# A Mamba layer with a mixture of experts: x * Dskip moves from a VectorE operation per half into the PSUM sum as a diagonal matmul

## The chip, the cores and the metric

The kernel runs on one core of a Trainium2 chip. The metric is the device time in microseconds. All operands are fp32 in memory. Besides the transfers there are four engines to follow: TensorE (PE in the profile, PEld for its weight loads), VectorE (DVE), ScalarE (ACT) and GpSimd (POOL).

## The reference

The input is (32, 256, 128), 8192 tokens. It is layer-normalised to xn, and the result is `x + mamba(xn) + moe(xn)`. Of the mamba part, this is what matters here (256 inner channels in two halves of 128, 16 states per channel):

```python
x = silu(conv(x) + conv_b)                    # xs in the kernel
delta = softplus(dt_proj(x_proj(x)) + dt_proj_b)
s = s * exp(delta * A) + (delta * x) * B      # a scan over 256 tokens
y = sum over the 16 states of s * C
y = y + x * Dskip
y = y * silu(z)                               # zs in the kernel
out = y @ out_proj_w.T
```

The mixture of experts sends each token to one of eight experts (128 to 512 to 128) and weighs it by its gate.

## The kernel before

After a start of some 95 us (weights, layernorm, routing) one loop runs over 16 chunks of 512 tokens, and in each over 32 slots, 16 to a half of the channels. The order of work on every engine is written out by hand: the tables `STAGE_A`, `OUT_PROJ`, `FFN_AT`, `SOFTPLUS` and `GATE` name the slots at which a piece of work is issued or read. Nothing is planned at run time; an engine does its list in order and waits at semaphores.

In slot w of a chunk:

- TensorE spreads the rows of du and delta over the partitions for slot w + 2, with one fp32r matmul each (`spread_du`, L1186, into `du_ps`, and `spread_delta`, L1193, into `decay`). The first waits until VectorE has read the bank's earlier content, the second until the scan of slot w - 1 is done. Behind them in its list come the sums over the states and the tiles of other work of that slot.
- ScalarE turns the spread delta into a decay with Exp (L808). Between these it does the SiLUs of the next chunk (L709, L711, each pair with two table loads), its softplus (L731 to L745) and the evacuations of the experts' tiles (L762, L768, L774, L784).
- VectorE multiplies the spread du by B (`spread_u`, L926) one slot ahead and scans (L991).
- GpSimd multiplies the scan's result by C (L615), and has the scaling of delta, its splitting into two parts and the indirect transfers between.

Every fourth slot TensorE sums four units over the states (`sum_quad`, L1208): four matmuls 128 x 32 side by side, each on its own 32 partitions of the bank `y_ps`. Four such sums, at slots 6, 10, 14 and 18 for half 0 and at 22, 26, 30 and 2 of the next chunk for half 1, fill the bank for one half. The first of the four opens the sum (`start`), and before it TensorE waits for `g_ready`, that is, until VectorE has read the bank's last half.

VectorE's `gate_half` has two steps for every half. Step 0 (L906) adds x * Dskip to the bank in place, step 1 (L910) multiplies by zs into `g_sb`. `GATE = (4, 5)` puts them in slots 20 and 21 for half 0, and in slots 4 and 5 of the next chunk for half 1:

```python
dve.scalar_tensor_tensor(y_ps[:, :], xs_of(ch, hf), dsk[:, hf:hf + 1], y_ps[:, :],
                         ALU.mult, ALU.add).then_inc(S["skip_added"], 1)
...
dve.wait_ge(S["skip_added"], per_chunk(ch, 2, hf + 1))
dve.tensor_tensor(g_sb[:, hf, :], y_ps[:, :], zs_of(ch, hf), ALU.mult
```

The output projection of a chunk (L1135) runs at slots 18 and 19 of the next chunk and reads `g_sb`; VectorE adds it to the result at slot 20 (`add_out`, L917), after step 0 of the gate of that slot. In the last chunk both steps and the output projection stand alone at the end.

The experts' work is laid into the chunks 1 to 12 in a pattern that repeats every three chunks: one block of tiles in chunks 1, 4, 7 and 10, two in 2, 5, 8 and 11, one in 3, 6, 9 and 12. L1153 and L1156 are an expert's two layers, L1150 and L1161 its transposes. L1101 and L1104 are the input projections of x and z of the next chunk, L1112 the projections of its xs, L1121 the assembling of its delta. GpSimd also issues the 64 indirect transfers that scatter the tokens (L622), all in chunks 0 and 1.

Of the kernel before, what the change touches and what calls it, by code (L numbers as in the profile page):

```python
# [23 lines left out]
ALU = mybir.AluOpType  # L24
# [3 lines left out]
P = 128  # L28
# [4 lines left out]
HALVES = DIN // P  # L33
CH = 512
CHUNKS = TOK // CH
# [4 lines left out]
UNITS = P // UC  # L40
SLOTS = HALVES * UNITS
QUADS = P // 32
# [13 lines left out]
W_LOADS = 9 + NS  # L56
# [40 lines left out]
            {"act": (25, 26, 27, 28), "scale": (31,), "zero": (32,), "high": (36,), "low": (34,), "low_dve": (35,)})  # L97
FIRST_SOFTPLUS = {"scale": 3, "zero": 4, "high": 7, "low": 7, "low_dve": 7}

GATE = (4, 5)  # L100
MOE_ADD_FROM, MOE_ADD_STEP, MOE_ADDS = 13 * 32 + 26, 4, 13


# [10 lines left out]
def bass_mamba_moe(nc, hidden, in_w, conv_w, conv_b, xp_w, dt_w, dt_b, a_log, d_skip, out_w,  # L114
                   wg, w1, b1, w2, b2, consts, out):
    ctx = ExitStack()
    with ctx:
        def sb(name, shape, dt=F32):
            return ctx.enter_context(nc.sbuf_tensor(name, shape, dt))

        def sem(name):
            return ctx.enter_context(nc.semaphore(name))
# [13 lines left out]
        ident = con[:, K_ID:K_ID + P]  # L136
# [10 lines left out]
        cw = small[:, 0:8].rearrange("p (h k) -> p h k", h=HALVES)  # L147
        cb, dtb, dsk = small[:, 8:10], small[:, 10:12], small[:, 12:14]
        neg_m, neg_t, log_t1, log_t2, neg_l0, none = (small[:, 14 + k:15 + k] for k in range(6))
        a_neg = sb("a_neg", [P, SLOTS])  # L150

        spot = [0]

        def over_xn(n):
# [26 lines left out]
        g_sb = sb("g_sb", [P, HALVES, CH])  # L181
# [31 lines left out]
        y_ps = bank[5]  # L213
# [4 lines left out]
        S = {n: sem(n) for n in (  # L218
            "x_loaded0 x_loaded1 x_loaded2 x_loaded3 con_loaded w_loaded xin_zeroed xin_loaded "
            "setup_dve setup_pe setup_act a_ready fill_zeroed fill_ready ein_filled moe_filled "  # L220
            "ln_act xn_ready xnT_pe xnT_act logits_pe route_dve route_act route_pe routed "
            "centred_dve centred_pool l0_ready var_ready rstd_ready xn_last lt_pe lt_act lg_read "
            "scattered du_spread delta_spread u_ready decay_ready scan_done p_dve p_ready sum_done "
            "skip_added g_ready misc_pe misc_act misc_dve misc_bc b_loaded0 b_loaded1 c_loaded0 c_loaded1 sp_act sp_chain "
            "dx_ready dd_ready hi_ready lo_ready stacked ffn_loaded0 ffn_loaded1 moe_put0 moe_put1 moe_put2 "
            "moe_put3 back_loaded0 back_loaded1 back_loaded2 back_loaded3 back_loaded4 back_loaded5 back_loaded6 "
            "back_loaded7 moe_added out_stored act_chain in_w_loaded").split()}
# [58 lines left out]
        def tile_bank(*key):  # L286
            return misc[find[key].bank]

        def tile_made(*key):

            return made[key]
# [23 lines left out]
        def softplus_now(t, what):  # L315

            return events.get((what, t), [])

        def per_chunk(ch, n, k):
            return ch * n + k  # L320
# [12 lines left out]
        def wait(eng, name, value):  # L333
            if not isinstance(value, int) or value > 0:
                eng.wait_ge(S[name] if isinstance(name, str) else name, value)

        def bc_loaded(ch, hf, kind):

            return S[f"{kind}_loaded{hf}"], per_chunk(ch, 32, 32)

        def xs_of(ch, hf):
            return xs[:, ch % 2, hf, :]

        def zs_of(ch, hf):
            return zs[:, ch % 2, hf, :]

        def head_of(w):

            return w % QUADS // 2
# [15 lines left out]
        def by_dve(ch, w):  # L365
            return w % QUADS < {0: HELP, CHUNKS - 1: HELP_LAST}.get(ch, 0)
# [15 lines left out]
        def decay_of(w):  # L382
            return decay[w % len(decay)]
# [451 lines left out]
        def _(dve):  # L835

            for b in range(LN_BLK):
                t = slice(b * BT, (b + 1) * BT)
# [46 lines left out]
            t = slice((LN_BLK - 1) * BT, TILES)  # L885
# [13 lines left out]

            def gate_half(ch, hf, step):

                if step == 0:
                    dve.wait_ge(S["sum_done"], per_chunk(ch, SLOTS // QUADS, UNITS // QUADS * (hf + 1)))
                    dve.scalar_tensor_tensor(y_ps[:, :], xs_of(ch, hf), dsk[:, hf:hf + 1], y_ps[:, :],  # L906
                                             ALU.mult, ALU.add).then_inc(S["skip_added"], 1)
                else:
                    dve.wait_ge(S["skip_added"], per_chunk(ch, 2, hf + 1))
                    dve.tensor_tensor(g_sb[:, hf, :], y_ps[:, :], zs_of(ch, hf), ALU.mult  # L910
                                      ).then_inc(S["g_ready"], 1)

            def add_out(ch):

                rows = acc[:, ch * CT:(ch + 1) * CT, :]
                dve.wait_ge(S["misc_pe"], tile_made("outp", ch, 0, 0))
                dve.tensor_tensor(rows, tile_bank("outp", ch, 0, 0)[:, :].rearrange("p (i d) -> p i d", d=DM), rows,  # L917
                                  ALU.add).then_inc(S["misc_dve"], 1)

            def spread_u(ch, w):  # L920

                hf = w // UNITS
                if w % UNITS == 0:
                    dve.wait_ge(*bc_loaded(ch, hf, "b"))
                dve.wait_ge(S["du_spread"], per_chunk(ch, SLOTS, w + 1))
                dve.tensor_tensor(u_sb[:, w % U_RING, :], du_ps[w % 2][:, :], b_of[:, hf, head_of(w), :], ALU.mult  # L926
                                  ).then_inc(S["u_ready"], 1)

            def split_low(ch, hf):

                dve.wait_ge(S["hi_ready"], per_chunk(ch, 2, hf + 1))
                dve.tensor_tensor(lo, dd, hi.bitcast(F32), ALU.subtract).then_inc(S["lo_ready"], 1)
# [47 lines left out]
            for ch in range(CHUNKS):  # L980
                for w in range(SLOTS):
                    t = ch * SLOTS + w
                    if w + 1 < SLOTS:
                        spread_u(ch, w + 1)
                    elif ch + 1 < CHUNKS:
                        spread_u(ch + 1, 0)
                    if w % QUADS == 0:
                        wait(dve, "sum_done", per_chunk(ch, SLOTS // QUADS, w // QUADS - 1))
                    dve.wait_ge(S["decay_ready"], t + 1)
                    dve.wait_ge(S["u_ready"], t + 1)  # L990
                    dve.tensor_tensor_scan(s_sb[:, w % S_RING, :], decay_of(w)[:, :], u_sb[:, w % U_RING, :], 0.0,  # L991
                                           ALU.mult, ALU.add).then_inc(S["scan_done"], 1)
                    if w > 0 and by_dve(ch, w - 1):
                        if w - 1 in (0, UNITS):
                            dve.wait_ge(*bc_loaded(ch, w // UNITS, "c"))
                        dve.wait_ge(S["scan_done"], t)
                        s_now = s_sb[:, (w - 1) % S_RING, :]
                        dve.tensor_tensor(s_now, s_now, c_of[:, (w - 1) // UNITS, head_of(w - 1), :], ALU.mult
                                          ).then_inc(S["p_dve"], 1)

                    for step in range(2):
                        if w == GATE[step] and ch > 0:
                            gate_half(ch - 1, 1, step)
                        if w == UNITS + GATE[step]:
                            gate_half(ch, 0, step)
                    for of, hf_, _ in softplus_now(t, "low_dve"):
                        split_low(of, hf_)
                    for x in reads_at.get(t, []):
                        if x.kind == "outp":
                            add_out(x.of)  # L1010

            gate_half(CHUNKS - 1, 1, 0)
            gate_half(CHUNKS - 1, 1, 1)
            add_out(CHUNKS - 1)


# [1 line left out]
        def _(pe):  # L1018
# [182 lines left out]
            def sum_quad(ch, k):  # L1201

                r = k % (UNITS // QUADS)
                if r == 0:
                    wait(pe, "g_ready", per_chunk(ch, 2, k * QUADS // UNITS))
                wait_products(pe, ch, QUADS * (k + 1))
                for q in range(QUADS):
                    mm = pe.matmul(y_ps[q * 32:(q + 1) * 32, :], con[:, K_SUM + 32 * r:K_SUM + 32 * (r + 1)],  # L1208
                                   s_sb[:, (QUADS * k + q) % S_RING, :],
                                   start=(r == 0), stop=(r == UNITS // QUADS - 1))  # L1210
                mm.then_inc(S["sum_done"], 1)

            def first_tile(kind, hf):
                x = find[(kind, 0, hf, 0)]
                for part in range({"x": TAPS, "D": 4}.get(kind, 1)):
                    tile_part(x, part)

            pe.wait_ge(S["xnT_act"], CHUNKS)
            first_tile("z", 0)
            first_tile("x", 0)  # L1220
            first_tile("bc", 0)
# [75 lines left out]
```

## Time and profile before

| | |
|---|---|
| runs (3) | median 1132.79 us, 1132.73 to 1134.38 |
| profiled execution | 1134.47 us, its span 1132.7 us |
| VectorE busy | 1028.1 us, 91% |
| TensorE busy | 965.9 us, 85%, mean granted clock 0.947 |
| GpSimd busy | 878.3 us, 78% |
| ScalarE busy | 755.8 us, 67% |

The profiled execution has 1.8 us around its span. A matmul's end is modelled and overlaps the start of the next, so that TensorE's busy share says less than the distance between the starts. An fp32 matmul is two records, an fp32r matmul one. The engines' clocks differ and each runs ahead of the others by some slots; a wait in one is therefore seen in another only if the lead is used up.

### The profile page before, as it was taken

Reading aid. Unit: us, or ns where it says so; the run is one execution under the profiler, and the core shown is the slowest. Engines: PE = TensorE matmul, PEld = TensorE weight load, DVE = VectorE, ACT = ScalarE, POOL = GpSimd, SP = SyncE. Lnnn points to the kernel's source line nnn. Section 1 sums busy time; section 2 is a strip of 40 time slices with the busy share of each in tenths; the row PEclk is TensorE's granted clock in tenths of the full one; section 3 lists DMA queues with packets and bytes.
Section 4 is the critical chain, followed back from the end, with each engine's and each line's share of the span. In section 5 each row is a group of like instructions: output and inputs, shape, how many; then the busy total and the mean of one; then the engine's idle time right before and its main releaser. Section 6 shows DMA issues by size and latency. Waiting matters only on the chain.

```text
span 1132.7 us, 11797 instructions
## 1 busy us (share of the span) xinstructions
PE 965.9 (85%) x3525; PEld 442.5 (39%) x3525; DVE 1028.1 (91%) x1227; ACT 755.8 (67%) x1197; POOL 878.3 (78%) x730
## 2 busy tenths in 40 slices
PE   0676667898999999999999899999999999788786
PEld 0432213344444444444444444444444444333232
DVE  6856887999999999999999999999999999999996
ACT  2574642768777687778786877768777878576331
POOL 3305888779888898888988989889888888888753
PEclk9998867999999999999999999999999999899766
DMA  7528353443353345244324335333524332855500
GB/s 170 178 37 230 99 117 70 99 100 79 77 120 79 79 84 117 44 82 113 71 61 112 83 77 119 77 81 76 125 42 83 75 65 65 200 118 112 131 28 10
DMA packets 76095, 107.23 MB, mean 95 GB/s; under 512 B 13528, under 2 KB 43136, under 8 KB 76032
## 3 DMA queue, kind: packets, MB, share of 16 engines
q1 hardware_dynamic: 71936, 98.02, 39.7%
q0 software_dynamic: 4096, 8.46, 2.2%
q8 instruction: 29, 0.48, 0.2%
q14 instruction: 34, 0.28, 0.1%
HBM read 18.24 MB, written 21.10 MB: 35 GB/s over the span
## 4 chain that ended last, share of the span: by engine, by line
PE 32%; DVE 24%; issue 16%; ACT 15%; POOL 10%; DMA 1%; SPq 1%; POOLq 0%; DVEq 0%; ACTq 0%
DVE u_sb L926 10%; DVE s_sb L991 8%; PE bank L1156 5%; PE bank L1193 4%; PE bank L1121 4%; POOL s_sb L615 4%; PE bank L1101 4%; POOL expert_in L622 4%; PE bank L1208 4%; PE bank L1186 3%; ACT bank L808 3%; PE bank L1153 3%; ACT L713 2%; ACT L709 2%; PE bank L1112 2%
## 5 line engine op out<-in xcount | busy, mean ns | idle before, releaser
L615 POOL TENSOR_TENSOR s_sb<-s_sb,c_of 128x512 f32<-128x512 f32 x480 | 614.2, 1289 | 135.8 <-DVE s_sb L991 131.2
L991 DVE TENSOR_TENSOR_SCAN s_sb<-bank,u_sb 128x512 f32<-128x512 f32 x512 | 620.9, 1213 | 14.7 <-ACT bank L808 14.2
L808 ACT ACTIVATE bank<-bank,a_neg 128x510 f32<-128x510 f32 x512 | 332.2, 663 | 212.2 <-PE bank L1193 210.6
L926 DVE TENSOR_TENSOR u_sb<-bank,b_of 128x512 f32<-128x512 f32 x512 | 343.7, 671 | 37.7 <-PE bank L1186 36.9
L1186 PE MATMUL bank<-dsp,sel_d 128*128 128x512 f32 x512 | 328.6, 642 | 32.8 <-DVE u_sb L926 20.2
L1193 PE MATMUL bank<-dsp,sel_d 128*128 128x512 f32 x512 | 230.3, 450 | 51.4 <-DVE s_sb L991 48.5
L1186 PEld LDWEIGHTS bank<-dsp,sel_d 128*128 128x128 f32 x512 | 101.0, 197 | 211.0 <-DVE u_sb L926 107.9
L1193 PEld LDWEIGHTS bank<-dsp,sel_d 128*128 128x128 f32 x512 | 101.2, 198 | 177.3 <-DVE s_sb L991 131.7
L1208 PE MATMUL bank<-s_sb,con 128*32 128x512 f32 x1024 | 147.8, 651 | 23.1 <-POOL s_sb L615 20.2
L1101 PE MATMUL bank<-xnT,wx 128*128 128x512 f32 x256 | 132.3, 602 | 0.0
L622 POOL DMA_INDIRECT expert_in<-xn,put_at x64 | 65.3, 1020 | 18.0 <-issue 17.8
L585 POOL DMA_INDIRECT moe<-xn x64 | 64.6, 1010 | 12.9 <-issue 9.2
L560 POOL TENSOR_TENSOR dd<-dd,xs 128x512 f32<-128x512 f32 x32 | 40.9, 1278 | 42.4 <-ACT dd L752 42.3
L1153 PE MATMUL bank<-xn 128*128 128x512 f32 x128 | 66.5, 611 | 4.7 <-ACT xn L762 4.7
L570 POOL TENSOR_TENSOR dd<-dd,hi 128x1024 fp32r<-128x1024 f32 x25 | 59.1, 2366 | 6.3 <-ACT hi L758 6.3
L1156 PE MATMUL bank<-xn 128*128 128x512 f32 x128 | 63.4, 602 | 0.0
L1101 PEld LDWEIGHTS bank<-xnT,wx 128*128 128x128 f32 x256 | 47.4, 191 | 26.7 <-issue 19.1
L768 ACT ACTIVATE xn<-bank,b1c 128x512 f32<-128x512 f32 x64 | 43.6, 700 | 18.8 <-PE bank L1153 18.8
L758 ACT ACTIVATE hi<-dd 128x1024 fp32r<-128x1024 f32 x32 | 33.7, 1053 | 31.7 <-POOL dd L564 31.7
L709 ACT ACT_TABLE_LOAD x32 | 41.1, 1283 | 14.6 <-PE bank L1104 14.3
L1208 PEld LDWEIGHTS bank<-s_sb,con 128*32 128x32 f32 x1024 | 21.1, 111 | 66.4 <-issue 49.2
L1121 PE MATMUL bank<-sp_e,con 128*128 128x512 f32 x64 | 36.5, 653 | 7.3 <-ACT xn L768 6.0
(144 smaller groups left out, 1034.4 us busy)
## 6 DMA issues: line engine op xcount, KB each, us to landing
b_of<-bc SPq DMA_DIRECT2D x64, 256.0 KB, 5.6
c_of<-bc SPq DMA_DIRECT2D x64, 256.0 KB, 6.0
dsp<-hi SPq DMA_DIRECT2D x64, 256.0 KB, 4.0
dsp<-dd SPq DMA_DIRECT2D x64, 256.0 KB, 4.6
expert_in<-fill SPq DMA_DIRECT2D x16, 260.0 KB, 3.3
xn<-expert_in SPq DMA_DIRECT2D x8, 520.0 KB, 5.3
moe<-fill SPq DMA_DIRECT2D x8, 512.0 KB, 6.5
xn<-L_ffn_W SPq DMA_DIRECT2D x16, 256.0 KB, 4.9
```

Of the source, the lines that this page charges most:

```text
L615: pool.tensor_tensor(s_now, s_now, c_of[:, hf, hh, :], ALU.mult).then_inc(S["p_ready"], 1)
L622: pool.indirect_dma_start(ein[:, :], bass.IndirectOffsetOnAxis(ap=put_at[:, i:i + 1], axis=0), xn_rows[:, i, :], None).then_inc(S["scatter ...
L808: act.activation(d, d, ACT.Exp, scale=a_neg[:, k:k + 1]).then_inc(S["decay_ready"], 1)
L926: dve.tensor_tensor(u_sb[:, w % U_RING, :], du_ps[w % 2][:, :], b_of[:, hf, head_of(w), :], ALU.mult).then_inc(S["u_ready"], 1)
L991: dve.tensor_tensor_scan(s_sb[:, w % S_RING, :], decay_of(w)[:, :], u_sb[:, w % U_RING, :], 0.0, ALU.mult, ALU.add).then_inc(S["scan_done" ...
L1101: mm = pe.matmul(t[:, :], wx[:, hf, part, :], xnT[:, seqs, part:part + SEQ], start=(part == 0), stop=(part == TAPS - 1))
L1121: pe.matmul(t[:, :], ident, (sp_e, sp_r, sp_a)[part], start=(part == 0), stop=False)
L1153: mm = pe.matmul(t[:, :], w1_sb[:, b, x.k * P:(x.k + 1) * P], xeT, start=True, stop=True)
L1156: mm = pe.matmul(t[:, :], w2_sb[:, b, part, :], hT[:, part, :], start=(part == 0), stop=(part == FT - 1))
L1186: pe.matmul(du_ps[w % 2][:, :], sel_d[:, group_of(w), :, :].rearrange("k n d -> k (n d)"), dsp[:, hf, head_of(w), 1, :], start=True, stop= ...
L1193: pe.matmul(decay_of(w)[:, :], sel_d[:, group_of(w), :, :].rearrange("k n d -> k (n d)"), dsp[:, w // UNITS, head_of(w), 0, :], start=True ...
L1208: mm = pe.matmul(y_ps[q * 32:(q + 1) * 32, :], con[:, K_SUM + 32 * r:K_SUM + 32 * (r + 1)], s_sb[:, (QUADS * k + q) % S_RING, :], start=(r ...
```

## The change

The weights of two diagonal matrices, diag(Dskip) for each half, are made once in the start. The first matmul of a half's sum is now a full 128 x 128 matmul of that diagonal with xs, with `start`; the 16 narrow ones of the four sums all accumulate. The gate is one operation, at slot 4 (20 for half 0), behind `add_out` where both fall in one slot.

```diff
-GATE = (4, 5)
+GATE = 4
...
+        skip_w = sb("skip_w", [P, HALVES, P])
...
-            def gate_half(ch, hf, step):
-
-                if step == 0:
-                    dve.wait_ge(S["sum_done"], per_chunk(ch, SLOTS // QUADS, UNITS // QUADS * (hf + 1)))
-                    dve.scalar_tensor_tensor(y_ps[:, :], xs_of(ch, hf), dsk[:, hf:hf + 1], y_ps[:, :],
-                                             ALU.mult, ALU.add).then_inc(S["skip_added"], 1)
-                else:
-                    dve.wait_ge(S["skip_added"], per_chunk(ch, 2, hf + 1))
-                    dve.tensor_tensor(g_sb[:, hf, :], y_ps[:, :], zs_of(ch, hf), ALU.mult
-                                      ).then_inc(S["g_ready"], 1)
+            dve.wait_ge(S["w_loaded"], 16 * W_LOADS)
+            for hf in range(HALVES):
+                dve.tensor_scalar(skip_w[:, hf, :], ident, dsk[:, hf:hf + 1], None, ALU.mult
+                                  ).then_inc(S["skip_ready"], 1)
+
+            def gate_half(ch, hf):
+
+                dve.wait_ge(S["sum_done"], per_chunk(ch, SLOTS // QUADS, UNITS // QUADS * (hf + 1)))
+                dve.tensor_tensor(g_sb[:, hf, :], y_ps[:, :], zs_of(ch, hf), ALU.mult
+                                  ).then_inc(S["g_ready"], 1)
...
-                    for step in range(2):
-                        if w == GATE[step] and ch > 0:
-                            gate_half(ch - 1, 1, step)
-                        if w == UNITS + GATE[step]:
-                            gate_half(ch, 0, step)
-                    for of, hf_, _ in softplus_now(t, "low_dve"):
-                        split_low(of, hf_)
                     for x in reads_at.get(t, []):
                         if x.kind == "outp":
                             add_out(x.of)
-
-            gate_half(CHUNKS - 1, 1, 0)
-            gate_half(CHUNKS - 1, 1, 1)
+                    if w == GATE and ch > 0:
+                        gate_half(ch - 1, 1)
+                    if w == UNITS + GATE:
+                        gate_half(ch, 0)
+                    for of, hf_, _ in softplus_now(t, "low_dve"):
+                        split_low(of, hf_)
+
+            gate_half(CHUNKS - 1, 1)
             add_out(CHUNKS - 1)
...
                 if r == 0:
-                    wait(pe, "g_ready", per_chunk(ch, 2, k * QUADS // UNITS))
+                    hf = k * QUADS // UNITS
+                    wait(pe, "g_ready", per_chunk(ch, 2, hf))
+                    pe.matmul(y_ps[:, :], skip_w[:, hf, :], xs_of(ch, hf), start=True, stop=False)
                 wait_products(pe, ch, QUADS * (k + 1))
...
-                                   start=(r == 0), stop=(r == UNITS // QUADS - 1))
+                                   start=False, stop=(r == UNITS // QUADS - 1))
...
             pe.wait_ge(S["xnT_act"], CHUNKS)
+            pe.wait_ge(S["skip_ready"], HALVES)
```

## Rows read from the trace of the kernel before

**Rows 1.** The page: the span, and each engine's busy time.

```profile
span 1132.7 us, 11797 instructions
...
PE 965.9 (85%) x3525; PEld 442.5 (39%) x3525; DVE 1028.1 (91%) x1227; ACT 755.8 (67%) x1197; POOL 878.3 (78%) x730
```

**Rows 2.** Busy time by stretch of 64 us: PE, PEld, DVE, ACT, POOL, PEclk, DMA.

```profile
553.00:617.00 64.00, 61.37 (x225) 28.51 (x226) 60.59 (x72) 48.65 (x78) 56.12 (x46) 1.00 0.41 89
...
1001.00:1065.00 64.00, 50.33 (x184) 21.34 (x184) 63.19 (x73) 40.97 (x62) 53.91 (x44) 0.96 0.44 94
```

**Rows 3.** Groups of instructions, shapes apart: busy us, mean ns | idle before.

```profile
L906 DVE SCALAR_TENSOR_TENSOR bank<-xs,small,bank 128x512 f32<-128x512 f32 x32 | 23.4, 730 | 3.6 <-PE bank L1208 3.6
...
L945 DVE TENSOR_REDUCE s_sb<-bank 128x16 f32<-128x128 f32 x4 | 1.2, 292 | 10.3 <-PE bank L1077 10.3
```

**Rows 4.** Timeline of DVE, chunk 4, slots 20 to 22: start us, us.

```profile
413.84 0.73 DVE L906 SCALAR_TENSOR_TENSOR bank<-xs,small,bank 128x512 f32<-128x512 f32 x1
414.48 0.68 DVE L917 TENSOR_TENSOR acc<-bank,acc 128x512 f32<-128x512 f32 x1
...
416.81 0.67 DVE L910 TENSOR_TENSOR g_sb<-bank,zs 128x512 f32<-128x512 f32 x1
417.39 0.68 DVE L926 TENSOR_TENSOR u_sb<-bank,b_of 128x512 f32<-128x512 f32 x1
```

**Rows 5.** The chain that ended last: first and last of 18 pieces on L906.

```profile
199.99 0.73 DVE bank L906
...
1097.31 0.02 DVE bank L906
```

**Rows 6.** The same chain in chunk 6, slots 22 to 27.

```profile
539.93 0.24 PE bank L1193
540.16 1.00 PE bank L1208 x8
...
542.68 0.87 PE bank L1112 x2
...
543.57 0.69 ACT sp_a L731
...
549.37 0.49 ACT xn L762
```

**Rows 7.** Timeline of PE, chunk 4, slots 22 to 27.

```profile
416.94 0.50 PE L1193 MATMUL bank<-dsp,sel_d 128*128 128x512 f32 x1 [0.18 <-DVE s_sb L991]
417.53 1.06 PE L1208 MATMUL bank<-s_sb,con 128*32 128x512 f32 x8
...
419.25 0.50 PE L1193 MATMUL bank<-dsp,sel_d 128*128 128x512 f32 x1 [0.24 <-DVE s_sb L991]
419.59 1.02 PE L1153 MATMUL bank<-xn 128*128 128x512 f32 x2
...
426.90 1.98 PE L1156 MATMUL bank<-xn 128*128 128x512 f32 x4
```

**Rows 8.** Timeline of ACT, chunk 4, slots 24 to 27.

```profile
421.51 0.69 ACT L731 ACTIVATE sp_a<-bank,small 128x512 f32<-128x512 f32 x1 [0.17 <-PE bank L1112]
...
426.16 1.27 ACT L768 ACTIVATE xn<-bank,b1c 128x512 f32<-128x512 f32 x2
```

**Rows 9.** Timelines of DVE and PE, chunk 4, slots 6 and 7.

```profile
388.60 1.22 DVE L991 TENSOR_TENSOR_SCAN s_sb<-bank,u_sb 128x512 f32<-128x512 f32 x1 [0.58 <-ACT bank L808]
...
387.49 0.49 PE L1193 MATMUL bank<-dsp,sel_d 128*128 128x512 f32 x1 [0.24 <-DVE s_sb L991]
387.92 1.07 PE L1112 MATMUL bank<-xs,bcw 128*64 128x512 f32 x2
```

**Rows 10.** Timelines of PE and DVE in chunk 15 and at the end.

```profile
1101.52 1.93 PE L1208 MATMUL bank<-s_sb,con 128*32 128x512 f32 x8 [0.69 <-DVE g_sb L910]
...
1122.80 0.76 DVE L906 SCALAR_TENSOR_TENSOR bank<-xs,small,bank 128x512 f32<-128x512 f32 x1 [3.58 <-PE bank L1208]
1123.59 0.69 DVE L910 TENSOR_TENSOR g_sb<-bank,zs 128x512 f32<-128x512 f32 x1
```

More of the change, by code:

```diff
@@ L223, in bass_mamba_moe @@
             "scattered du_spread delta_spread u_ready decay_ready scan_done p_dve p_ready sum_done "
-            "skip_added g_ready misc_pe misc_act misc_dve misc_bc b_loaded0 b_loaded1 c_loaded0 c_loaded1 sp_act sp_chain "
+            "skip_ready g_ready misc_pe misc_act misc_dve misc_bc b_loaded0 b_loaded1 c_loaded0 c_loaded1 sp_act sp_chain "
             "dx_ready dd_ready hi_ready lo_ready stacked ffn_loaded0 ffn_loaded1 moe_put0 moe_put1 moe_put2 "
```

## The prediction, made before the changed kernel was run

> **What bounds the kernel now.** I read the page first: VectorE is busy 91% of the span, TensorE 85% [rows 1]. By stretches VectorE has 60.6 of 64 us in the middle and 63.2 near the end [rows 2]. So it looks like VectorE's kernel, and the 32 skip operations of 0.73 us, 23.4 us in all, look like what can be had [rows 3]. But an average does not say which wait ends last, so I read the chain of waits next. The skip operation lies on it in only 18 of 32 halves [rows 5]; where it doesn't, the chain runs through TensorE and ScalarE, with VectorE at most 3 us a chunk idle and yet not in command. The question for each half is therefore: who arrives second, and by how much?
>
> **The change part by part.**
>
> *Removed from VectorE.* From the skip operation's start to the next start is 0.64 us (413.84 to 414.48), from the gate's 0.58 [rows 4]. So a half gives back 0.64 us of VectorE, 20.5 us over 32, if nobody else comes late.
>
> *Added to TensorE.* One fp32 matmul 128 x 128 x 512 per half. Its nearest rows are the same shape in the chain: 0.87 us for the two records of L1112 [rows 6]. At full clock I take 0.87, in all 27.8 us; at the low of the two clock levels, where a sum of four units takes 1.93 us instead of 1.00 [rows 6, 10], twice that. It is queued behind the two spreads of slot 6 or 22 and ahead of that slot's sum, the next slot's spreads and every tile behind them; ScalarE's decays and softplus wait for those. The narrow matmuls keep their number and shape; that they accumulate I cost at nothing (the other three sums of each half do so already, at the same length).
>
> *Moved.* The gate goes from slot 21 to 20 (5 to 4), so `g_ready` comes one slot earlier and TensorE's wait for it before the sum goes. In slot 20 `add_out` now stands ahead of the gate and its wait for the output projection is no longer covered by the skip operation; in chunk 4 it began without a wait right after it [rows 4], and the projection's matmuls belong to slots 18 and 19, so I cost it at nothing in the middle. If the cover is gone, it costs at most the 0.64 us that the change gave.
>
> *Start.* Two operations on 128 columns, less than 0.73 us each [rows 3]. They lie ahead of the routing, where VectorE is idle 10.3 us for TensorE's transposes [rows 3]. Nothing; at most 1.4 us if that cover were gone.
>
> Now the halves, by who is second:
>
> 1. *Half 0 of chunks 3, 6, 9, 12 (4 halves).* The chain runs through TensorE without a gap at slot 22: spread, sum, tiles, L1112, then ScalarE's softplus at 543.57 and on to its L762 at 549.37, all back to back [rows 6]. VectorE isn't on it, so its 0.64 us buys nothing and the new matmul is paid in full: 4 x 0.87 = +3.5 us. Bounds 0 (if the time is hidden) and 4 x 1.74 (low clock) = +7.0; by stretch the clock is 1.00 there [rows 2], hence 0.87.
> 2. *Half 0 of 1, 2, 4, 5, 7, 8, 10, 11 (8 halves).* Here VectorE is on the chain at slot 20. In chunk 4 TensorE's spread at 416.94 waits for a scan that becomes 0.05 us earlier (the gate takes the skip operation's place, 0.58 for 0.64). Then 0.34 us until the next matmul can start (as 419.25 to 419.59 [rows 7]), skip 0.87, sum 1.00, two spreads at 0.24 each: 416.89 + 0.34 + 0.87 + 1.00 + 0.48 = 419.58. The tile behind them began at 419.59 [rows 7]. VectorE's scan would have let it begin 0.64 earlier; TensorE has used that up to within 0.01 us. A later spread does come 0.64 earlier, but the next tiles wait for ScalarE, which is back to back from 421.51 (fed by the tile that did not move) to 426.16; TensorE's L1156 begins at 426.90 as the first of that pair ends [rows 7, 8]. Gain 0. Bounds: 8 x -0.64 = -5.1, and the excess of rival B.
> 3. *Half 1 of 3, 6, 9, 12, gated in the next chunk (4).* ScalarE's SiLUs delay the decay, and the scan at 388.60 waits 0.58 us for it [rows 9]; 0.64 us saved before it becomes 0.64 more idle. TensorE's 0.24 us wait before 387.49 [rows 9] is where the gain can show: 0.1 each, -0.4; bounds 0 and -0.64 each.
> 4. *Half 1 of 1, 2, 4, 5, 7, 8, 10, 11 (8).* Not on the chain, the same ScalarE stretch: 0.
> 5. *Chunk 0 (2).* GpSimd's scattering holds the chain over half 0: 0. Half 1, at 199.99 [rows 5], is VectorE's: -0.64 at most, -0.3 taken.
> 6. *Chunks 13 and 14 (4).* No experts; VectorE is at 63.2 of 64 [rows 2], TensorE at 50: the full 0.64, -2.6.
> 7. *Chunk 15 (2).* Half 0 comes at the low clock: the sum takes 1.93 us [rows 10] and the skip would take some 1.7, more than the wait of 0.69 it fills. 0, bounds -0.6 and +0.7. Half 1 stands alone at the end: the gate starts at once, 1123.59 - 1122.80 = 0.79 [rows 10]: -0.8.
>
> Sum: +3.5 - 0.4 - 0.3 - 2.6 - 0.8 = **-0.6 us**. The profiled execution took 1134.47 us, 1.7 over the median of 1132.79; the sum is a difference within it, so I put it against the median: **1132.2 us**.
>
> **The rivals.**
>
> *A. VectorE commands wherever the chain names it.* Then 17 of the 18 halves give 0.64 (-10.9), the last half 0.8, chunk 3's kind still costs 3.5: -8.2, 1124.6 us. For it: the chain's own rows [rows 5]. Against: the tie to 0.01 us worked out in 2. Its extreme is VectorE as the bound everywhere, 20.5 + 0.2 us, 1112.1 us; the busy shares [rows 1] speak for it, 14 halves off the chain against it. The Trainium skill (Perfetto Trace Analysis, Identifying the Most-Contended Engine) would have this one: occupancy names the engine to relieve, and that is VectorE here. I give 0.18 to A and 0.04 to the extreme.
>
> *B. Slower: TensorE pays more than 0.87 in slot 22.* The step from a full-width matmul to the narrow ones in the same bank may not overlap as it does behind a spread. One of the two passes laid bare is 0.43 us. It would hit the 4 halves of case 1 and the 8 of case 2, which have no slack left: 12 x 0.43 - 0.6 = +4.6, 1137.4 us. It decides from 0.24 us a half (12 x 0.24 - 0.6 = +2.3). For it: from a spread to a sum TensorE takes 0.23 in the chain [rows 6] with nothing to drain but one pass. Against: in those rows the switch costs no more than a spread does. Chance 0.17. The Trainium skill (TensorEngine Tiling (Array Packing), Key Properties) says that changing the tiling mode drains the engine. By that rule the 256 changes that the sums make already stay the same in number, since the skip is full-width like the spread before it; only what is drained gets longer.
>
> *C. The change does less than it says* (the skip hidden in the wait for `g_ready` that it replaces, the gate's wait taking the skip's place): 0, 1132.8 us. Chance 0.03.
>
> **How the numbers follow.** My forecast has 0.58. An error of 2 us in its sum is likely, as most terms are zeros between bounds: 0.46 of it stays within 0.2%, 0.10 is faster, 0.02 slower. The 0.2% is 2.3 us, about what measurements of this kernel tell from no change. Faster: 0.10 + 0.18 + 0.04 = 0.32, with rounding 0.33. Slower: 0.17 + 0.02 = 0.19. Same: 0.46 + 0.03 = 0.49, rounded to 0.48. The range goes from A's 1124.5 to B's 1137.5; it leaves out the extreme and the worst clock.
>
> **What would show it.** L906 gone, 64 records of a new matmul from the diagonal at L1205's place, about 0.87 us a pair; VectorE's busy time down by some 23 us while its idle time for TensorE (L926) and ScalarE (L991) goes up by nearly as much; of every three chunks in the middle one longer by some 0.9 us and two unchanged; chunks 13 and 14 shorter by some 1.3 us each; no wait for `g_ready` before the sums. The prediction is wrong if the middle chunks get shorter by 0.6 us or more, or if the pair takes clearly over 0.87 before the sum starts.

## The result and the profile after

The changed kernel takes **1137.61 us** (median of 7 runs, 1136.57 to 1145.79) against 1134.07 for the kernel before (7 runs, 1132.73 to 1135.15): ratio 1.0046, interval 1.0028 to 1.0063. It is slower by 3.5 us by the medians, 5.2 by the ratio. Its runs also spread over 9.2 us where those of before spread over 2.4. The longest of them, 1145.79 us, had a mean granted clock of 0.913 where the other six had 0.948 or 0.949.

The page of the changed kernel: span, busy time, the chain that ended last.

```profile
span 1134.8 us, 11896 instructions
...
PE 981.4 (86%) x3589; PEld 448.7 (40%) x3589; DVE 1007.8 (89%) x1197; ACT 756.0 (67%) x1197; POOL 879.4 (77%) x730
...
PE 42%; DVE 18%; ACT 14%; issue 12%; POOL 12%; DMA 1%; SPq 1%; POOLq 0%; DVEq 0%; ACTq 0%
```

VectorE lost 20.3 us of busy time (1028.1 in [rows 1]). TensorE's share of the chain went from 32% to 42%, VectorE's from 24% to 18%. The groups, with shapes apart, of the scan (L992, before L991), of u (L927, before L926), of the gate, and of the new matmul:

```profile
L992 DVE TENSOR_TENSOR_SCAN s_sb<-bank,u_sb 128x512 f32<-128x512 f32 x512 | 620.3, 1212 | 27.6 <-ACT bank L809 23.3 <-issue 3.9
L927 DVE TENSOR_TENSOR u_sb<-bank,b_of 128x512 f32<-128x512 f32 x512 | 342.9, 670 | 48.6 <-PE bank L1185 48.3
L1206 PE MATMUL bank<-xs,skip_w 128*128 128x512 f32 x64 | 35.9, 646 | 0.0
L911 DVE TENSOR_TENSOR g_sb<-bank,zs 128x512 f32<-128x512 f32 x32 | 21.4, 670 | 3.6 <-PE bank L1209 3.6
```

The work did what the diff says: 64 records from the diagonal, and TensorE never waits in front of them. The idle time before L992 and L927 is 76.2 us; the two groups had 14.7 and 37.7 in the kernel before. That is 23.8 us more, a little over what was taken off VectorE. What was saved there became waiting for TensorE and ScalarE.

**By chunk.** The start of slot 0's scan in chunks 6, 7, 8 and 9, in VectorE's timeline of the changed kernel:

```profile
498.64 1.22 DVE L992 TENSOR_TENSOR_SCAN s_sb<-bank,u_sb 128x512 f32<-128x512 f32 x1
560.59 1.21 DVE L992 TENSOR_TENSOR_SCAN s_sb<-bank,u_sb 128x512 f32<-128x512 f32 x1
622.09 1.22 DVE L992 TENSOR_TENSOR_SCAN s_sb<-bank,u_sb 128x512 f32<-128x512 f32 x1
684.55 1.21 DVE L992 TENSOR_TENSOR_SCAN s_sb<-bank,u_sb 128x512 f32<-128x512 f32 x1
```

The same four scans in the kernel before:

```profile
498.17 1.22 DVE L991 TENSOR_TENSOR_SCAN s_sb<-bank,u_sb 128x512 f32<-128x512 f32 x1
559.23 1.21 DVE L991 TENSOR_TENSOR_SCAN s_sb<-bank,u_sb 128x512 f32<-128x512 f32 x1
620.43 1.22 DVE L991 TENSOR_TENSOR_SCAN s_sb<-bank,u_sb 128x512 f32<-128x512 f32 x1
682.71 1.21 DVE L991 TENSOR_TENSOR_SCAN s_sb<-bank,u_sb 128x512 f32<-128x512 f32 x1
```

Chunk 6 takes 61.95 us instead of 61.06, chunk 7 61.50 instead of 61.20, chunk 8 62.46 instead of 62.28. The pattern of three repeats: call chunks 4, 7, 10 kind A, 2, 5, 8, 11 kind B, 3, 6, 9, 12 kind C. Read in this way, each kind is longer by about the same amount in each of its chunks: A 0.29 to 0.30, B 0.15 to 0.18, C 0.86 to 0.89. **Two chunks are not like their kind**: 9 and 12 take 63.63 and 63.64 us, 1.7 more than 3 and 6. That is in no term of the prediction.

**Where the 1.7 us comes from.** The windows of the changed kernel around slot 27 of chunk 9: PE, PEld, DVE, ACT, POOL, PEclk, DMA.

```profile
733.00:737.00 4.00, 2.25 (x12) 0.72 (x11) 4.00 (x6) 4.00 (x11) 3.16 (x3) 1.00 0.05 18
737.00:741.00 4.00, 3.75 (x6) 1.68 (x7) 1.49 (x2) 3.02 (x7) 3.64 (x4) 0.57 0.04 16
```

TensorE is busy 2.25 of 4 us, and in the next 4 us its granted clock is 0.57 of full: it stands at the lower of its two levels, 1.2 GHz instead of 2.4, for 3.4 us. TensorE's timeline, the same place in chunk 6 (first two rows) and chunk 9:

```profile
549.20 0.45 PE L1192 MATMUL bank<-dsp,sel_d 128*128 128x512 f32 x1
551.36 1.96 PE L1152 MATMUL bank<-xn 128*128 128x512 f32 x4 [1.72 <-ACT xn L763]
...
735.08 0.45 PE L1192 MATMUL bank<-dsp,sel_d 128*128 128x512 f32 x1
737.25 3.65 PE L1152 MATMUL bank<-xn 128*128 128x512 f32 x4 [1.72 <-ACT xn L763]
```

In both, TensorE has waited 1.72 us for ScalarE's L763. In chunk 6 the four records behind it take 1.96 us, in chunk 9 3.65: the difference is the 1.7 us. The kernel before at the same place:

```profile
548.37 0.46 PE L1193 MATMUL bank<-dsp,sel_d 128*128 128x512 f32 x1
550.00 1.96 PE L1153 MATMUL bank<-xn 128*128 128x512 f32 x4 [1.16 <-ACT xn L762]
```

Its wait is 1.16 us, 1.18 in the other three chunks of the kind, and its clock never falls between chunks 2 and 12. So there were two questions for the runs: is the matmul's price in the chunks what the terms say, and does the rest come from the clock behind a longer wait?

### The profile page after: what moved, and what is told of

The parts are those of the page before. It is cut to its first block, busy times and chain, and to the rows that moved or that the text cites. A ratio compares the mean times of both kernels' runs of the same rounds, so it can differ in the third digit from the quotient of the medians.

```text
span 1134.8 us, 11896 instructions
## 1 busy us (share of the span) xinstructions
PE 981.4 (86%) x3589; PEld 448.7 (40%) x3589; DVE 1007.8 (89%) x1197; ACT 756.0 (67%) x1197; POOL 879.4 (77%) x730
## 4 chain that ended last, share of the span: by engine, by line
PE 42%; DVE 18%; ACT 14%; issue 12%; POOL 12%; DMA 1%; SPq 1%; POOLq 0%; DVEq 0%; ACTq 0%
DVE u_sb L927 7%; DVE s_sb L992 7%; PE bank L1209 6%; PE bank L1192 5%; POOL expert_in L623 5%; PE bank L1155 5%; PE bank L1185 5%; PE bank L1120 4%; PE bank L1100 4%; PE bank L1152 4%; POOL s_sb L616 4%; ACT bank L809 3%; PE bank L1111 2%; PE bank L1134 2%; PE bank L1206 2%
## 5 line engine op out<-in xcount | busy, mean ns | idle before, releaser
L992 DVE TENSOR_TENSOR_SCAN s_sb<-bank,u_sb 128x512 f32<-128x512 f32 x512 | 620.3, 1212 | 27.6 <-ACT bank L809 23.3
L927 DVE TENSOR_TENSOR u_sb<-bank,b_of 128x512 f32<-128x512 f32 x512 | 342.9, 670 | 48.6 <-PE bank L1185 48.3
L1185 PE MATMUL bank<-dsp,sel_d 128*128 128x512 f32 x512 | 327.1, 639 | 29.8 <-DVE u_sb L927 16.9
L1192 PE MATMUL bank<-dsp,sel_d 128*128 128x512 f32 x512 | 224.6, 439 | 46.3 <-DVE s_sb L992 42.7
L1209 PE MATMUL bank<-s_sb,con 128*32 128x512 f32 x1024 | 145.0, 640 | 15.5 <-POOL s_sb L616 15.4
L1152 PE MATMUL bank<-xn 128*128 128x512 f32 x128 | 70.2, 642 | 8.6 <-ACT xn L763 6.9
L586 POOL DMA_INDIRECT moe<-xn x64 | 64.6, 1010 | 14.7 <-issue 7.8
L1155 PE MATMUL bank<-xn 128*128 128x512 f32 x128 | 63.4, 602 | 0.0
L710 ACT ACT_TABLE_LOAD x32 | 41.1, 1283 | 14.7 <-PE bank L1103 14.3
```

Source lines behind the costliest of these rows:

```text
L1152: mm = pe.matmul(t[:, :], w1_sb[:, b, x.k * P:(x.k + 1) * P], xeT, start=True, stop=True)
L1155: mm = pe.matmul(t[:, :], w2_sb[:, b, part, :], hT[:, part, :], start=(part == 0), stop=(part == FT - 1))
L1185: pe.matmul(du_ps[w % 2][:, :], sel_d[:, group_of(w), :, :].rearrange("k n d -> k (n d)"), dsp[:, hf, head_of(w), 1, :], start=True, stop= ...
L1192: pe.matmul(decay_of(w)[:, :], sel_d[:, group_of(w), :, :].rearrange("k n d -> k (n d)"), dsp[:, w // UNITS, head_of(w), 0, :], start=True ...
```

## The experiments

The kernel before had medians of 1133.56 (first four runs, 12 times) and 1134.14 us (last four, 22 times) beside them.

**1. The changed kernel again**, no edit.

> The changed kernel once more, for the spread and a second profile. Theory 1 (the loss is TensorE's serial time in slot 22 and the same in every execution): slower than before by 3 to 5 us, and the times of its slots differ from the first profile by less than 0.2 us a chunk wherever the granted clock is full. Theory 2 (the loss is mostly the TensorE clock, which falls in some executions while TensorE waits for ScalarE in slots 27 and 28): the profile has its half-clock stretches in the middle chunks at other places than chunks 9 and 12, or none, and each moves that chunk by about 1.7 us.

Measured: 1138.59 us (1134.35 to 1141.97, 7 runs), ratio 1.0048, 1.0031 to 1.0064. The slowdown is real. This time the profile has chunks 9 and 12 at 61.94 and 61.93 us and chunks 3 and 6 at 63.57 and 63.31. In chunk 6 of this run:

```profile
554.40 3.14 PE L1152 MATMUL bank<-xn 128*128 128x512 f32 x4 [1.72 <-ACT xn L763]
```

The same wait of 1.71 to 1.72 us stands in all four chunks of both executions, and the slow matmuls behind it in two of the four, not the same two. So it is chance per execution, not the place. It explains a part of the spread between runs and not all of it. Both profiled executions have two such chunks, and yet this one is 2.0 us longer; its chunks 0 and 1 together take 158.0 us where they took 155.6 in the first, and why stays open. And four such drops of the clock, at 1.7 us each, are 6.8 us, less than the run of 1145.79 us has over the kernel before.

**2. The matmul alone.** The kernel before with the diagonal matmul, VectorE's operation kept but with a scalar of zero (`none`).

```diff
-                    dve.scalar_tensor_tensor(y_ps[:, :], xs_of(ch, hf), dsk[:, hf:hf + 1], y_ps[:, :],
+                    dve.scalar_tensor_tensor(y_ps[:, :], xs_of(ch, hf), none, y_ps[:, :],
...
+                    pe.matmul(y_ps[:, :], skip_w[:, hf, :], xs_of(ch, hf), start=True, stop=False)
```

> The added matmul alone: VectorE keeps its operation in its place, with a scalar of zero. Theory 1: TensorE is behind at slot 22 of every middle chunk by 0.87 us with nothing won on VectorE: chunks 3, 6, 9, 12 longer by 0.9 us as in the changed kernel, the other middle chunks longer by 0.5 to 0.9 us instead of 0.15 to 0.29; in all 8 to 14 us slower than before. Theory 2: near the changed kernel's loss in the middle, within 2 us of it, with half-clock stretches. Rival 3 (the matmul hides and the gate's new place costs): no slower than before.

Measured: 1150.03 us (4 runs), ratio 1.0148, 1.0133 to 1.0163: +16.5 us. Chunks of kind C take 61.95 us, +0.88, just what they take with the whole change (one of the four, chunk 12, has the lower clock and takes 63.66): there the matmul is paid in full and VectorE's saving is worth nothing. Kinds A and B are longer by 1.13 and some 0.6 us. The total is above the 8 to 14 us expected.

**3. The operation removed alone.** The changed kernel without the matmul, so that x * Dskip is missing from its result.

```diff
-                    pe.matmul(y_ps[:, :], skip_w[:, hf, :], xs_of(ch, hf), start=True, stop=False)
...
-                                   start=False, stop=(r == UNITS // QUADS - 1))
+                                   start=(r == 0), stop=(r == UNITS // QUADS - 1))
```

> The removed operation alone: x * Dskip is left out of the output, no matmul is added, the gate is the one operation of the changed kernel. Theory 1: VectorE's 0.64 us goes through in the tail (chunks 13 to 15, -3.5 us) and in half 0 of chunks 2, 5, 8, 11 for a part, and is taken by waits for ScalarE elsewhere: -4 to -8 us. If VectorE really commanded, -11 us (the 18 halves on the chain) or -20 us (all of them). Theory 2 adds half-clock stretches in the middle, since TensorE has more idle time: then less is won, -1 to -3 us.

Measured: 1123.89 us (1122.68 to 1128.43, 6 runs), ratio 0.9929, 0.9912 to 0.9945: -9.7 us, more than the 4 to 8 expected and about half of the 20.5 that VectorE gives back. By chunk: A 60.44 (-0.77), B 61.64 (-0.64), C 61.08 (0). So VectorE does command kinds A and B, for one half or a little more in each chunk, and kind C not at all. In kinds A and B the matmul takes this gain away in the changed kernel and costs 0.15 to 0.3 us more; in kind C it adds all of its time.

**4. The matmul moved.** A sum in PSUM takes its terms in any order, so half 1's matmul need not open the sum in slot 22; the narrow matmuls of that slot open it instead. Here it accumulates later, where TensorE waits for ScalarE or has room: slot 24, 29 and 27 in kinds A, B and C.

```diff
+            def skip_slot(ch):
+                return {1: 24, 2: 29, 0: 27}[ch % 3] if 1 <= ch <= 12 else 24
...
+                    if hf == 0:
+                        skip(ch, 0)
...
+                    if w == skip_slot(ch):
+                        skip(ch, 1)
```

> The same work, but for half 1 the diagonal matmul no longer opens the sum in slot 22; it accumulates in a slot in which TensorE waits (24 in chunks 1, 4, 7, 10; 29 in 2, 5, 8, 11; 27 in 3, 6, 9, 12). Theory 1: chunks 3, 6, 9, 12 lose their 0.9 us, half of the removed operation's time shows in 2, 5, 8, 11: 4 to 7 us faster than before. Theory 2: no half-clock stretch in the middle, as the matmul fills the wait; -1.7 us for each that the changed kernel had. If the narrow matmuls behind a wide one are what costs, the first slot of each half 1 is back at its old length and the summing in the next one longer.

Measured: 1124.66 us (1123.68 to 1124.88, 5 runs), ratio 0.9919, 0.9907 to 0.9932: 13 to 14 us faster than the changed kernel, 9 faster than the kernel before (4 to 7 were expected), with all the work of the change. Kinds A, B, C take 60.72, 61.64 and 61.10 us. TensorE's timeline in chunk 4 and at the wait of chunk 6:

```profile
416.43 0.49 PE L1185 MATMUL bank<-dsp,sel_d 128*128 128x512 f32 x1
416.76 0.46 PE L1192 MATMUL bank<-dsp,sel_d 128*128 128x512 f32 x1
417.05 1.02 PE L1152 MATMUL bank<-xn 128*128 128x512 f32 x2
...
544.98 1.02 PE L1201 MATMUL bank<-xs,skip_w 128*128 128x512 f32 x2
546.86 1.95 PE L1152 MATMUL bank<-xn 128*128 128x512 f32 x4 [0.87 <-ACT xn L763]
```

Counted from its chunk's first scan, L1152 in chunk 4 begins at 44.39 us, where it began at 44.90 in the kernel before (L1153, at 419.59) and at 45.18 in the changed one (at 419.90). In chunk 6 the wait for ScalarE is 0.87 us instead of 1.72, the matmul standing in it, and no chunk from 2 to 12 has the lower clock.

**5. Useless work in the wait.** The changed kernel with one matmul more: identity times xs into a free bank, in slot 27 of kind C, ahead of the tile that waits for ScalarE. Its result is overwritten.

```diff
+                        if w == 27 and ch in (3, 6, 9, 12) and x.kind == "h" and x.bank == 1:
+                            y = find[("h", x.of, x.hf, x.k + 1)]
+                            claim(y)
+                            pe.matmul(misc[y.bank][:, :], ident, xs_of(ch, 1), start=True, stop=True)
```

> The changed kernel, and in slot 27 of chunks 3, 6, 9 and 12 one more full-width matmul (the identity with xs, into a bank that is overwritten next), in the wait of 1.7 us that TensorE has there for ScalarE. Theory 2 (the clock falls in and after that wait, and each time costs 1.7 us): no half-clock stretch in the middle, chunks 3, 6, 9, 12 at 61.95 us each though TensorE does more, and runs that spread by 2 us instead of 7: 2 to 4 us faster than the changed kernel, 0 to 2 us slower than before. Theory 1 (the loss is serial time only): as slow as the changed kernel, or slower by what the matmul adds.

Measured: 1134.36 us (1133.02 to 1137.04, 11 runs), ratio 1.0005, 0.9997 to 1.0014. It does 3.5 us more of TensorE's work than the changed kernel and is 3.3 to 4.2 us faster; the intervals of the two ratios do not meet. Chunk 9 of this kernel, which had the lower clock in the first profile of the changed one:

```profile
735.55 1.02 PE L1253 MATMUL bank<-xs,con 128*128 128x512 f32 x2
737.43 1.96 PE L1152 MATMUL bank<-xn 128*128 128x512 f32 x4 [0.86 <-ACT xn L763]
```

The wait is 0.86 us, the four records behind it take 1.96, and so in all four chunks. Every chunk from 1 on takes what it takes in the profile of the changed kernel within 0.05 us, except 9 and 12, which are 1.7 us shorter each. Nothing but the clock is different there. Two to two and a half drops an execution, at 1.7 us each, would make the difference of the medians; each of the two profiles of the changed kernel has two. The runs of this kernel still spread over 4.0 us where 2 were expected, so something else varies too.

**6. The matmul moved, but not into the wait.** As experiment 4, with slot 24 in kind C too; the diff is against that kernel.

```diff
-                return {1: 24, 2: 29, 0: 27}[ch % 3] if 1 <= ch <= 12 else 24
+                return {1: 24, 2: 29, 0: 24}[ch % 3] if 1 <= ch <= 12 else 24
```

> As the kernel with the matmul moved, but in chunks 3, 6, 9 and 12 it stands in slot 24 instead of 27, ahead of the wait for ScalarE instead of in it. If where it stands matters only by the lateness of the tiles that ScalarE waits for: those are issued in slot 23, so chunk 3's kind stays at 61.1 us. If the filling of the wait keeps the clock (theory 2): the wait is back to 1.2 us or more and some of these chunks have a half-clock stretch, 1.7 us each; the median 0 to 4 us over the moved kernel's 1124.7 us.

Measured: 1126.49 us (1125.50 to 1127.43, 5 runs), 1.8 us more than experiment 4. Chunks 3 and 6 take 61.09 and 61.08 us, as there: out of slot 22 the matmul is free. But the wait in slot 27 is 1.68 us again, and chunks 9 and 12 have the lower clock and take 62.21 and 62.40. TensorE in chunk 9:

```profile
728.67 0.40 PE L1192 MATMUL bank<-dsp,sel_d 128*128 128x512 f32 x1
730.74 2.87 PE L1152 MATMUL bank<-xn 128*128 128x512 f32 x4 [1.68 <-ACT xn L763]
```

The excess is 1.1 and 1.3 us here, less than in the changed kernel.

**7. Both halves' matmuls moved.** As experiment 4, and half 0's opens the sum at the end of slot 5; the diff is against that kernel.

```diff
             def skip(ch, hf):
+                if hf == 0:
+                    wait(pe, "g_ready", per_chunk(ch, 2, 0))
...
+                    if w == 5:
+                        skip(ch, 0)
```

> As the kernel with the matmul moved, and for half 0 it opens the sum at the end of slot 5, ahead of the spreads of slot 6, where TensorE waits 0.4 to 0.8 us for a scan, instead of behind them. Chunks 4, 7, 10, 13 lose the 0.28 us that they have over the kernel without a matmul; if slot 8 of chunks 1 and 14 (+1.15 us in each) comes from the same place, these go too: 1 to 3 us faster than the moved kernel.

Measured: **1122.07 us** (1121.49 to 1122.91, 4 runs), ratio 0.9892, 0.9877 to 0.9906: the fastest of all, 12 us ahead of the kernel before. All three kinds take what they take with no matmul at all (experiment 3), kind A 60.44 us, and chunk 1 falls from 68.44 to 67.29 us. The page of this kernel:

```profile
span 1121.1 us, 11896 instructions
...
PE 975.7 (87%) x3589; PEld 449.1 (40%) x3589; DVE 1006.4 (90%) x1197; ACT 756.1 (67%) x1197; POOL 879.8 (78%) x730
```

Number and shape of all instructions are those of the changed kernel (11896 in both, the counts by engine the same); only where TensorE runs 32 pairs of them differs, and it is worth 16 us.

**8. The gate a slot later.** The changed kernel with `GATE = 5`.

```diff
-GATE = 4
+GATE = 5
```

> The changed kernel with its one gate operation in slots 5 and 21, where the second step stood, instead of 4 and 20. The matmul then waits for the gate behind the scan of slot 21, as the sum did before. If the new place of the gate matters (the matmul may start 0.6 us earlier): each middle half costs up to 0.6 us more in slot 22, 5 to 10 us slower than the changed kernel. If it is only the matmul's own length that counts: within 1.5 us of the changed kernel.

Measured: 1135.87 us (1134.69 to 1140.89, 11 runs), ratio 1.0024, 1.0014 to 1.0035: 1.7 to 2.7 us less than the changed kernel, with intervals that meet. Kind A takes 61.01 us (0.5 less than with the gate in slot 4), kind B 62.28 (0.2 less), kind C the same; chunks 13, 14 and the tail give back 3.9 us against the first profile of the changed kernel, 3.0 against experiment 1's. The chunks of kind C still have a wait of 1.72 us, and chunk 9 the lower clock. So the move of the gate by itself is a trade between the middle and the end, and not the cause of the slowdown.

**The clock over all profiles.** In kind C's slot 27 the wait was 1.68 to 1.73 us in six profiles (the changed kernel's two, experiments 2, 3, 6 and 8): 24 waits, and 8 of them were followed by the lower clock. In four (before, experiments 4, 5 and 7) it was 0.85 to 1.18 us: 16 waits, none followed by it. Either half of the change alone is enough for the long wait: it is 1.73 with the matmul alone and 1.72 to 1.73 with the operation alone removed. In experiment 3's profile none of its four was followed by a drop, although two of its six runs were 4 us above the rest. A drop made its chunk longer by 1.1 to 1.7 us. What makes the difference between one execution and the next isn't settled.

## Why the prediction was wrong

It gave 1132.2 us and a chance of 0.19 for slower; 1137.6 lies 0.1 us outside its range. Of the 5.4 us between them 1.3 is its base: it put the sum against 1132.79, the median of three runs, and the kernel before has 1134.1 over 22. The rest is the change itself: -0.6 said, +3.5 measured. The scans' starts of the two profiles give every term of its sum:

| term of the prediction | said | measured |
|---|---|---|
| 1, half 0 of chunks 3, 6, 9, 12 | +3.5 | +3.5 |
| 2, half 0 of eight chunks | 0 | +1.2 |
| 3, half 1 of 3, 6, 9, 12 | -0.4 | +0.6 |
| 4, half 1 of eight chunks | 0 | 0 |
| 5, chunk 0 | -0.3 | 0.0 |
| 6, chunks 13 and 14 | -2.6 | -3.6 |
| 7, chunk 15 and the end | -0.8 | -1.9 |
| sum | -0.6 | -0.2 |
| the clock in two chunks of kind C | not there | +3.4 |

The spans differ by 2.1 us, these two lines and -1.1 us ahead of the first scan, which changes from one profile to the next (93.8 to 95.8 us in the ten). In this profile the sum was right to 0.4 us, in part by luck: terms 2 and 3 erred one way and 6 and 7 the other. With experiment 1's profile the same seven rows add up to +3.1, since chunks 0 and 1 take 2.4 us more there and 13 and 14 some 0.9 more. Experiment 5 rests on more runs: with the waits of kind C filled, the changed kernel is at +0.2 us (-0.3 to +1.6) where the prediction said -0.6. What it has over that, 3.3 to 4.2 us, is the clock.

**What failed is the step that costs a matmul in kind C with the clock as given**: "by stretch the clock is 1.00 there [rows 2], hence 0.87". The stretch of [rows 2] begins at 553, behind the slots 22 to 27 of chunk 6. The one that holds them, in the kernel before:

```profile
489.00:553.00 64.00, 58.70 (x224) 27.32 (x222) 61.35 (x74) 49.43 (x82) 55.23 (x46) 1.00 0.41 89
```

It has 1.00 too, with a wait of 1.16 us in it. That is the clock behind the wait as it was; the prediction put the clock behind the new one at the same level, and did not ask how long the wait would be after the change. It became 1.72 us: ScalarE's L763 comes 0.89 us later in its chunk, for the matmul, and TensorE reaches the wait only some 0.35 us later: its waits for scans on the way there, 0.24 and 0.54 us before, have become one of 0.29. In the two profiles of the changed kernel the clock fell behind 4 of its 8 such waits, and the four matmuls there took 3.14 to 3.65 us instead of 1.96. Its words for the wrong clock ("leaves out ... the worst clock") were about the new matmul itself at half speed, not about the work behind a wait.

Point by point.

*Term 1* is right and shown three times: +0.88 with the matmul alone, 0 with it left out, 0 with it moved out of slot 22. The chain of the changed kernel in chunk 6 is the one of [rows 6] with the matmul ahead of it:

```profile
544.04 0.87 PE bank L1111 x2
...
544.93 0.69 ACT sp_a L732
...
550.73 0.50 ACT xn L763
551.22 0.14 issue
551.36 1.96 PE bank L1152 x4
```

L732 begins 1.36 us later than at 543.57, of which 0.47 is chunk 6's later start and 0.89 the matmul and its switch; L763 and L1152 follow with the same 1.36.

*Term 2* ended as a tie, as said, but the tie was 0.15 us a half off. TensorE in chunk 4, the rows that answer to [rows 7]:

```profile
417.06 0.50 PE L1192 MATMUL bank<-dsp,sel_d 128*128 128x512 f32 x1
417.39 1.02 PE L1206 MATMUL bank<-xs,skip_w 128*128 128x512 f32 x2
418.34 1.07 PE L1209 MATMUL bank<-s_sb,con 128*32 128x512 f32 x8
419.34 0.50 PE L1185 MATMUL bank<-dsp,sel_d 128*128 128x512 f32 x1
419.67 0.39 PE L1192 MATMUL bank<-dsp,sel_d 128*128 128x512 f32 x1
419.90 1.02 PE L1152 MATMUL bank<-xn 128*128 128x512 f32 x2
```

From the spread to L1152 it is 2.84 us where the prediction worked out 2.69. Two steps are longer: from the matmul to the sum 0.95 instead of 0.87, and from the spread behind the sum to the next spread 0.33 instead of 0.24. Both stood in the trace of the kernel before, a few lines away: there L1153 at 414.31 is followed by the narrower L1112 at 415.26, 0.95 later, and after the sum in chunk 6 the spreads begin at 548.04 and 548.37. Whoever works out a tie to 0.01 us has to take each step from a row with the same neighbours.

*Term 3* has the same excess. TensorE in slot 6 of chunk 4:

```profile
385.48 1.02 PE L1206 MATMUL bank<-xs,skip_w 128*128 128x512 f32 x2
386.43 1.06 PE L1209 MATMUL bank<-s_sb,con 128*32 128x512 f32 x8
387.43 0.50 PE L1185 MATMUL bank<-dsp,sel_d 128*128 128x512 f32 x1
387.77 0.40 PE L1192 MATMUL bank<-dsp,sel_d 128*128 128x512 f32 x1
388.09 1.07 PE L1111 MATMUL bank<-xs,bcw 128*64 128x512 f32 x2
```

The wait of 0.24 us before the spread of [rows 9] is gone, as expected, but it is more than filled: L1111 begins 0.17 us later than at 387.92 (0.03 of it from before the chunk). The gain of 0.1 that the term took was the room before the matmul; the matmul took all of it. With the matmul in slot 5 this is given back (experiment 7).

*Term 5*: the gate of chunk 0's half 1 comes when the clock is at its lower level; the matmul's pair has 1.63 us and the sum 1.94 behind it, and the 0.5 us by which chunk 0 is shorter are lost again in chunk 1, in the slots behind it. In experiment 1's profile of the same kernel the term is +2.4, so one profile says little about it.

*Term 6* was right in kind; this profile has -3.6, experiment 1's the -2.6 that was said. A gate in slot 20 leaves more than its 0.64 us: in slot 22 of chunks 13 and 14 VectorE is 1.3 us earlier. With the gate back in slot 21 these chunks lose most of their gain (63.20 and 62.86 us before, 61.46 and 60.73 changed, 62.80 and 61.94 in experiment 8), so it is the place of the gate, not the removed operation alone. Which of the operations in slot 21 it no longer stands in front of wasn't tried. Both kernels also have stretches at the lower clock in these chunks (the granted clock is 0.60 of full from 974 to 978 us before and 0.57 from 986 to 990 changed), and what they cost there isn't separated.

*Rival A* was half right. That VectorE commands where the chain names it is shown by experiment 3 for kinds A and B, and without its 3.5 us for the matmul it has -11.7, against a gain of 9.7 us with no matmul (experiment 3) and 12.1 with all of them moved (experiment 7). It failed here since the matmul stood on the same path. Its extreme is refuted: some 20 us less of VectorE gave 9.7 to 12.1. The Trainium skill's rule in Perfetto Trace Analysis, Identifying the Most-Contended Engine, calls the engine with the highest occupancy the one to optimise first. Here relieving VectorE gave about half of the time taken off it, and shortened seven of the eleven middle chunks.

*Rival B* gave 1137.4 us, which is almost the measured time, but its mechanism did not bring it. The excess of the switch is 0.08 us at the matmul and 0.09 behind the sum, under the 0.24 from which it decides and far from its 0.43. The rule that changing the mode drains TensorE (the Trainium skill, TensorEngine Tiling (Array Packing), Key Properties) agrees with these rows in sign, at a price of 0.08 us.

## What to carry over

An operation moved from one engine to another is worth what its new place costs: the same 32 matmuls and the same removed operation made this kernel some 4 us slower with the matmuls at the head of a sum and 12 us faster with them in slots where TensorE waits or has room, and an accumulation lets one choose the place. When a change moves TensorE and the work it waits for by different amounts, ask how long the wait becomes and what that does to TensorE's clock, and look in the windows behind it in more than one execution. Where a kernel's runs spread more than before, compare equal chunks within one profile: that is how the stall that comes by chance was found here.

## What the runs showed that was not expected

- A TensorE wait of 1.7 us in an otherwise full stretch was followed by 3.4 us at 1.2 GHz in 8 of 24 cases, and cost 1.1 to 1.7 us each time; waits of 0.85 to 1.18 us were never followed by it in 16.
- A matmul whose result nobody reads made the kernel 3.3 to 4.2 us faster, by cutting that wait from 1.72 to 0.86 us.
- A full-width fp32 pair is followed by narrow matmuls after 0.95 us and by full-width ones after 0.86; a spread right behind a sum is followed by the next after 0.33 to 0.34 us, in a row of full-width matmuls after 0.23 to 0.24.
